# Layer 0's first six steps in orders of their own, bulk loads behind single fetches, and U's and V's split weights first

## The chip, the core and the metric

The kernel runs on one core of one Trainium2 chip. Its time is the device time in microseconds (us) of one execution; the number compared is the median of several runs. One execution was also recorded by the hardware profiler, and every row below is from that one.

## What is computed

The reference takes 32 sequences of 256 token numbers, fetches each token's row of 192 numbers from a table, adds a position row, and runs four layers of a gated recurrence; then one layer of attention with 12 heads and one quantised product. The change touches the fetch and the start of the four layers:

```
x = embedding[tokens] + pos_enc[:S][None]
for l in range(L):                      # L = 4
    h = layernorm(x) * g + b
    uv = h @ Wi.T + bi ; u, v = uv[..., :D], uv[..., D:]        # D = 192
    uc = dwconv_causal(u, cw, cb)                               # 4 taps
    delta = softplus(uc @ wd.T + bd); Bm = uc @ wB.T + bB; Cm = uc @ wC.T + bC
    h_t = h_{t-1} * exp(-delta) + uc * Bm ; y = sum(h_t * Cm)   # over the sequence
    x = x + (y * sigmoid(v)) @ wo.T + bo
```

## The kernel before

The 8192 rows are cut into 16 chunks of two sequences (4 tiles of 128 rows each). Each layer walks over the 16 chunks, and x stays on the chip throughout, so chunk n of layer l+1 needs only chunk n of layer l. The kernel is written with one hand-ordered program for each engine; semaphores tie them together. All of them go through the same sequence of steps (`steps`): in step k of layer 0, `at(j)` is chunk k - j, so one step works on several chunks at different stages. The first six steps and the last few of a layer are written out, those between run in a loop.

The stages of a chunk n, with the engine that does each:

- `index(n)` and `gather(n)`, GpSimd: copies four columns of row numbers and issues four indirect DMAs that fetch the chunk's rows into the buffer `emb`. For the first four chunks (`FIRST`) each has a slot of its own; later chunks reuse slots 0 and 1, and `index(n)` waits until chunk n - 2 was taken out of its slot.
- `place(n)`, VectorE: waits for the fetch, adds the position rows and writes x. `statistics` and `variance` follow.
- `inverse_deviation(n)`, GpSimd: seven small operations that make `rstd`, one of them a power.
- `round_rows(n)`, ScalarE, and `rest_of_rows(n)`, VectorE: the scaled rows `xs`, rounded, and what the rounding left.
- `transposes(n)`, TensorE, and `save_turned(n)`, ScalarE: `xs` turned into `ht`.
- `uv(n)`, TensorE: 15 products with `w_uv` and `w_uv_rest`. `save_u` and `first_tap` on ScalarE and `other_taps` on VectorE make the convolution `uc`; `gates` on ScalarE makes sigmoid(v), `sv_l` and `sv_h`. TensorE's next `uv` waits for the gates of the chunk before, since the banks are the same.
- `round_uc` (ScalarE) and `rest_of_uc` (VectorE), then TensorE's `z_c` and `b_c` with `w_z`, `decay` on ScalarE, `recurrence` on VectorE, `rows` on TensorE, `residual` on VectorE. `bias_rows(n)` on GpSimd adds the output bias to x.

Each layer's weights are prepared one layer ahead: TensorE's `means`, then `centre_weights` (VectorE), `round_weights` (ScalarE) and `split_weights` (VectorE), which computes what rounding left of the weights. For layer 0 this is done ahead of the first step, for layer 1 in steps 2 to 5 of layer 0 (`means(1)` at the end of step 3, once gates(1) is done and layer 1's weights are loaded).

The SyncE program issues the plain loads, in order. After layer 0's weights it waits for the first two fetches, then issues w_o, the four bias rows, all constants of the attention stage and, once `split_weights(0)` is done, layer 1's weights.

## Time and profile before

| | |
|---|---|
| median of 3 runs | 1627.1 us (1626.98 to 1628.12) |
| the profiled execution: its time, its span | 1625.93 us, 1624.1 us |
| TensorE busy | 1522.8 us, 94% of the span |
| VectorE busy | 1345.7 us, 83% |
| ScalarE busy | 1241.7 us, 76% |
| GpSimd busy | 775.8 us, 48% |
| TensorE's mean granted clock | 0.971 of full speed |

The span goes from the first to the last instruction. A row of the waits says who waited for whom, and how long in all. A row of a timeline has the start, the duration, the engine, the line in the kernel, the operation, the tile written and the tile read, how many instructions were merged, and in brackets how long the engine had been idle before it and what ended that. "us to landing" is from a DMA's issue to its completion.

### The profile page before, as it was taken

To read this page: it belongs to the slowest core of one execution; us is meant where nothing else is said; L and a number is where in the kernel's file an instruction comes from. 1 tells how busy PE (TensorE), PEld (TensorE's weight loads), DVE (VectorE), ACT (ScalarE), POOL (GpSimd) and SP (SyncE) were. 2 spreads that over 40 slices of the span, in tenths; PEclk is the share of its full clock that TensorE was granted. 3 is DMA by queue.
4 is the path that set the end of the run, shared out by engine and by line. 5 is a ranking of instruction groups with operands and counts; after the bars stand their busy time and mean duration, and the time that the engine had idled before them with its cause. 6 is when DMAs were issued, how large, how long until landed. Compare 5 with 4: busy or idle time off the path is not lost.

```text
span 1624.1 us, 36462 instructions
## 1 busy us (share of the span) xinstructions
PE 1522.8 (94%) x11337; PEld 1242.0 (76%) x11337; DVE 1345.7 (83%) x3231; ACT 1241.7 (76%) x2686; POOL 775.8 (48%) x1386
## 2 busy tenths in 40 slices
PE   2699999999999999999999998899999999999995
PEld 2478788888888888888788887677777777777763
DVE  4589999889999899999799986678878888788763
ACT  2577878788888788888788884678877878788873
POOL 6655643223333223333233325666666666666542
PEclk9799999999999999999999998899999999999996
DMA  6111110000000000000000000000000000000000
GB/s 156 30 28 22 29 65 1 1 33 0 0 1 1 1 1 0 0 1 1 1 1 0 1 1 1 3 2 17 12 10 10 10 15 11 10 10 10 16 12 25
DMA packets 16572, 22.42 MB, mean 14 GB/s; under 512 B 2912, under 2 KB 13792, under 8 KB 16480
## 3 DMA queue, kind: packets, MB, share of 16 engines
q1 hardware_dynamic: 13408, 14.98, 2.8%
q0 software_dynamic: 3072, 6.30, 2.3%
q8 instruction: 48, 0.79, 0.2%
q14 instruction: 44, 0.36, 0.1%
HBM read 14.58 MB, written 6.29 MB: 13 GB/s over the span
## 4 chain that ended last, share of the span: by engine, by line
PE 41%; ACT 22%; DVE 19%; issue 14%; POOL 2%; DVEq 1%; DMA 1%; ACTq 0%; POOLq 0%
PE banks L861 7%; PE banks L829 6%; PE banks L786 5%; PE banks L813 5%; DVE x L1465 5%; ACT xs L1104 4%; ACT ht L1094 4%; PE banks L800 4%; DVE xs L1376 4%; ACT dc_l L1079 2%; PE banks L637 2%; DVE hs_h L1428 2%; DVE inp_h L1419 2%; PE banks L772 2%; ACT u_h L1050 2%
## 5 line engine op out<-in xcount | busy, mean ns | idle before, releaser
L1521 DVE TENSOR_REDUCE mx<-banks 128x4 f32<-128x1024 f32 x192 | 234.1, 1219 | 44.8 <-PE banks L800 44.2
L1152 ACT ACTIVATE probs<-banks 128x1024 f32<-128x1024 f32 x192 | 195.8, 1020 | 85.3 <-PE banks L813 82.0
L460 POOL TENSOR_TENSOR x<-x,bo_row 128x768 f32<-128x768 f32 (+1 forms) x64 | 118.8, 1856 | 191.6 <-DVE ucr_r L1402 191.6
L637 PE MATMUL banks<-ht,w_uv 128*128 128x512 f32 x576 | 171.8, 408 | 19.5 <-ACT sv_l L1127 13.7
L436 POOL TENSOR_TENSOR lnt<-mv,const 128x4 f32<-128x4 f32 x64 | 20.5, 321 | 315.6 <-DVE mv L1367 315.5
L637 PEld LDWEIGHTS banks<-ht,w_uv 128*128 128x128 f32 x576 | 111.3, 197 | 50.0 <-issue 18.3
L1393 DVE SCALAR_TENSOR_TENSOR uc_h<-u_h,vec,uc_h 128x512 f32<-128x512 f32 x192 | 143.8, 749 | 3.6 <-ACT uc_h L1065 3.6
L1376 DVE SCALAR_TENSOR_TENSOR xs<-x,rstd,xs 128x192 fp32r<-128x192 f32 x256 | 90.0, 413 | 63.8 <-ACT xs L1104 63.8
L1044 ACT ACTIVATE u_l<-banks,vec 64x256 f32<-64x256 f32 x128 | 60.0, 469 | 87.6 <-PE banks L637 86.8
L637 PE MATMUL banks<-ht,w_uv_rest 128*128 128x512 f32 x384 | 122.7, 402 | 0.0
L1061 ACT ACTIVATE uc_l<-banks,vec 64x256 f32<-64x256 f32 x128 | 71.8, 561 | 58.3 <-DVE inp_l L1422 57.2
L813 PE MATMUL banks<-q_t,k_t 64*128 64x256 f32 x768 | 108.9, 333 | 7.0 <-ACT probs L1152 5.1
L646 PE MATMUL banks<-ucr_h,w_z 128*128 128x512 f32 x256 | 107.7, 421 | 6.1 <-ACT ht L1094 5.3
L786 PE MATMUL banks<-identr,parts 128*128 128x128 f32 x768 | 104.3, 260 | 3.9 <-issue 3.0
L1094 ACT ACTIVATE ht<-banks 128x512 fp32r<-128x512 f32 x192 | 100.8, 598 | 4.8 <-PE banks L698 3.3
L698 PEld LDWEIGHTS banks<-identr,xs 128*128 128x128 f32 x768 | 73.8, 142 | 39.7 <-DVE xs L1376 18.1
L1104 ACT ACTIVATE xs<-x,rstd 128x192 fp32r<-128x192 f32 (+1 forms) x256 | 95.6, 444 | 10.8 <-POOL rstd L448 9.2
L829 PE MATMUL banks<-probs,v_aug 128*32 128x256 f32 x1536 | 103.6, 388 | 0.1
L698 PE MATMUL banks<-identr,xs 128*128 128x128 f32 x768 | 76.3, 247 | 29.1 <-DVE xs L1376 18.0
L646 PE MATMUL banks<-ucr_l,w_z 128*128 128x512 f32 x256 | 100.9, 394 | 0.0
L727 PE MATMUL banks<-w_o,sv_h 128*128 128x192 f32 x512 | 100.8, 341 | 0.0
L646 PE MATMUL banks<-ucr_l,w_z_rest 128*128 128x512 f32 x256 | 100.7, 393 | 0.0
(181 smaller groups left out, 4605.2 us busy)
## 6 DMA issues: line engine op xcount, KB each, us to landing
out_dram<-y_out SPq DMA_DIRECT2D x32, 192.0 KB, 2.0
raw_z<-w_z_dram SPq DMA_DIRECT2D x4, 704.0 KB, 6.1
raw_uv<-w_uv_dram SPq DMA_DIRECT2D x4, 576.0 KB, 4.9
emb<-embedding_dram,idx POOLq DMA_INDIRECT x64, 3.6
q_t<-mx_t SPq DMA_DIRECT2D x64, 6.0 KB
emb<-w_qkv_dram SPq DMA_DIRECT2D x1, 864.0 KB, 5.0
w_o<-w_o_dram SPq DMA_DIRECT2D x1, 768.0 KB, 5.5
bo_row<-bout_dram SPq DMA_DIRECT2D x4, 96.0 KB, 7.2
```

What stands on the lines that cost most here:

```text
L637: last = nc.tensor.matmul(out[:], w, r[:], start=(k == 0), stop=(k == len(passes) - 1))
L646: last = nc.tensor.matmul(out[:], w, r[:, b, :], start=(k == 0), stop=(k == len(passes) - 1))
L698: last = nc.tensor.transpose(B_T[g][:, k * P:(k + 1) * P].bitcast(F32R), xs[:, k, g * P:(g + 1) * P], identr[:])
L786: last = nc.tensor.transpose(B_HEADS[g][:, (2 * o + t) * P:(2 * o + t + 1) * P].bitcast(F32R), parts[:, s, t, o, 2 * g:2 * g + 2, :].rearr ...
L813: last = nc.tensor.matmul(B_ST[j][:, t * S:(t + 1) * S], k_t[q, s, g, t * P:(t + 1) * P], q_t[q, s, g, :], start=True, stop=True)
L829: last = nc.tensor.matmul(bank[32 * h:32 * h + 32, c:c + S], v_aug[:, s, t, 4 * p + h, :], probs[:, (s + p) % 2, h // 2, (2 * (h % 2) + t) ...
L1094: last = act.activation(ht[g][:], B_T[g][:], ACT.Identity)
L1104: last = act.activation(xs[:, k, 0:D], x[:, tile_of(c, k)], ACT.Identity, scale=rstd[:, s, k:k + 1])
L1152: act.activation(probs[:, (s + g // 2) % 2, g % 2, :].rearrange("p (j k) -> p j k", j=2), B_SST, ACT.Exp, scale=float(DH) ** -0.5).then_in ...
L1376: last = nc.vector.scalar_tensor_tensor(out=xs[:, k, D:2 * D], in0=x[:, tile_of(c, k)], scalar=rstd[:, s, k:k + 1], in1=xs[:, k, 0:D].bitc ...
L1393: nc.vector.scalar_tensor_tensor(out=uc, in0=uk, scalar=v(l, part, V_W0 + k), in1=uc, op0=ALU.mult, op1=ALU.add).then_inc(taps, 1)
L1521: nc.vector.tensor_reduce(mx[:, s].rearrange("p t (j h) -> p j t h", j=2)[:, :, :, g], B_SS.rearrange("p j (t k) -> p j t k", t=2), AX, AL ...
```

## The change

Four things change, all of them ahead of or within steps 0 to 5 of layer 0; the loops and all later layers keep their order, except that each layer's `split_weights` does U's and V's part first.

1. SyncE: the bias row of layer 0 is loaded behind fetch 1, w_o behind fetch 2, and everything else, layer 1's weights included, behind fetch 3.
2. GpSimd: only fetches 0 to 2 are issued up front, with `inverse_deviation(0)` behind fetch 1 and ahead of fetch 2. In steps 0 to 5 `inverse_deviation(k + 1)` comes ahead of `gather(k + 3)`, and `index(k + 4)` comes last.
3. ScalarE: a first sigmoid on one column stands ahead of everything; layer 0's `w_z` is rounded first, then chunk 0's rows, then `w_uv`; in step 2 gates(0) and round_uc(0) come ahead of round_rows(2).
4. VectorE: steps 0 to 2 have an order of their own (below); in steps 3 to 5 `place(k + 2)` moves from the start of the step to its end. `split_weights` makes `w_uv_rest` first, and TensorE's `uv` waits for these two alone, its `z_c` for all four.

```diff
-            for n in range(2):
-                sp.wait_ge(s_emb[n], 16 * CT)
+            sp.wait_ge(s_emb[1], 16 * CT)
+            sp.dma_start(bo_row[:, 0, :], bout[0:1, :].broadcast_to([P, D])).then_inc(s_bo, 16)
+            sp.wait_ge(s_emb[2], 16 * CT)
             sp.dma_start(w_o[:], w_o_d).then_inc(s_wo, 16)
-            for i in range(L):
+            sp.wait_ge(s_emb[3], 16 * CT)
+            for i in range(1, L):
                 sp.dma_start(bo_row[:, i, :], bout[i:i + 1, :].broadcast_to([P, D])).then_inc(s_wo, 16)
...
-            inverse_deviation(item(0))
+            for n in range(FIRST - 1):
+                wait(pool, s_idx4, n + 1)
+                gather(n, n, n % 2)
+                if n == 1:
+                    pool.wait_ge(s_zero, 3)
+                    inverse_deviation(item(0))
...
+                if l == 0 and k is not None and k < OPENING:
+                    inverse_deviation(at(-1))
+                    if k == 0:
+                        wait(pool, s_idx4, FIRST)
+                    gather(fetched[0], fetched[2], fetched[3])
+                    bias_rows(at(0))
+                    index(indexed[0], indexed[2], indexed[3])
...
                 if first_of_layer(it):
-                    pe.wait_ge(w_split, 4 * (l + 1))
+                    pe.wait_ge(w_split, 4 * l + 2)
...
+            act.activation(table[:], ident[:, 0:1], ACT.Sigmoid)
...
-            round_weights(0)
+            round_z(0)
+            round_rows(item(0))
+            round_uv(0)
...
+                if l == 0 and k == 2:
+                    gates(at(2))
+                    round_uc(at(2))
+                    round_rows(at(0))
...
+            place_and_measure(0)
             centre_weights(0)
+            rest_of_rows(item(0))
+            place_and_measure(1)
             split_weights(0)
...
+                opening = l == 0 and k is not None and k < OPENING
+                if opening and k == 0:
+                    place_and_measure(2)
+                    rest_of_rows(item(1))
+                    return
+                if opening and k == 1:
+                    return
+                if opening and k == 2:
+                    other_taps(at(2), (0, 1, 2))
+                    rest_of_uc(at(2), 1)
+                    rest_of_uc(at(2), 0)
+                    place_and_measure(3)
+                    rest_of_rows(at(0))
+                    place(4, 4, 0)
+                    spread_gain(1)
+                    return
...
                 residual(at(4))
+                if opening:
+                    place(it[0], it[2], it[3])
```

VectorE's program before, from `place(0)` on; `raw_uv` is centring, `w_z_rest` and `w_uv_rest` are the split, `xs` is rest_of_rows(0):

```order
L1332 TENSOR_TENSOR x<-emb,pos 128x768
L1352 BN_STATS stats<-x 128x6 x4
L1367 BN_AGGR mv<-stats 128x2 x4
L1332 TENSOR_TENSOR x<-emb,pos 128x768
L1287 SCALAR_TENSOR_TENSOR raw_uv<-raw_uv,gain,banks 128x384 x3
...
L1307 TENSOR_TENSOR w_z_rest<-raw_z,w_z 128x704 x2
L1310 TENSOR_TENSOR w_uv_rest<-raw_uv,w_uv 128x384 x2
L1332 TENSOR_TENSOR x<-emb,pos 128x768
L1352 BN_STATS stats<-x 128x6 x4
L1367 BN_AGGR mv<-stats 128x2 x4
L1376 SCALAR_TENSOR_TENSOR xs<-x,rstd,xs 128x192 x4
```

The same place in the changed program:

```order
L1368 TENSOR_TENSOR x<-emb,pos 128x768
L1388 BN_STATS stats<-x 128x6 x4
L1403 BN_AGGR mv<-stats 128x2 x4
L1323 SCALAR_TENSOR_TENSOR raw_uv<-raw_uv,gain,banks 128x384 x3
...
L1412 SCALAR_TENSOR_TENSOR xs<-x,rstd,xs 128x192 x4
L1368 TENSOR_TENSOR x<-emb,pos 128x768
L1388 BN_STATS stats<-x 128x6 x4
L1403 BN_AGGR mv<-stats 128x2 x4
L1343 TENSOR_TENSOR w_uv_rest<-raw_uv,w_uv 128x384 x2
L1346 TENSOR_TENSOR w_z_rest<-raw_z,w_z 128x704 x2
L1368 TENSOR_TENSOR x<-emb,pos 128x768
```

Centring no longer stands behind the wait for fetch 1, and rest_of_rows(0) no longer behind the wait for fetch 2.

VectorE's program in step 2 and at the start of step 3, before; the first row is `place(4)`, `uc_l` and `uc_h` are chunk 0's taps, `ucr_l` and `ucr_r` its rest_of_uc, and the last two rows are `place(5)` and chunk 5's statistics:

```order
L1332 TENSOR_TENSOR x<-emb,pos 128x768
L1352 BN_STATS stats<-x 128x6 x4
L1393 SCALAR_TENSOR_TENSOR uc_l<-u_l,vec,uc_l 128x256
...
L1393 SCALAR_TENSOR_TENSOR uc_h<-u_h,vec,uc_h 128x512
L1376 SCALAR_TENSOR_TENSOR xs<-x,rstd,xs 128x192 x4
L1407 TENSOR_TENSOR ucr_l<-uc_l,ucr_l 64x256 x2
L1402 TENSOR_TENSOR ucr_r<-uc_h,ucr_h 128x512
L1279 TENSOR_SCALAR gain_rows<-gain 128x128 x2
L1332 TENSOR_TENSOR x<-emb,pos 128x768
L1352 BN_STATS stats<-x 128x6 x4
```

The same place in the changed program; the two `x` rows are `place(3)` and `place(4)`, and the last row is chunk 4's statistics, the start of step 3:

```order
L1429 SCALAR_TENSOR_TENSOR uc_l<-u_l,vec,uc_l 128x256
L1429 SCALAR_TENSOR_TENSOR uc_h<-u_h,vec,uc_h 128x512
L1443 TENSOR_TENSOR ucr_l<-uc_l,ucr_l 64x256 x2
L1438 TENSOR_TENSOR ucr_r<-uc_h,ucr_h 128x512
L1368 TENSOR_TENSOR x<-emb,pos 128x768
L1388 BN_STATS stats<-x 128x6 x4
L1403 BN_AGGR mv<-stats 128x2 x4
L1412 SCALAR_TENSOR_TENSOR xs<-x,rstd,xs 128x192 x4
L1368 TENSOR_TENSOR x<-emb,pos 128x768
L1315 TENSOR_SCALAR gain_rows<-gain 128x128 x2
L1388 BN_STATS stats<-x 128x6 x4
```

Chunk 0's taps have nothing ahead of them in step 2 now, and the whole of step 3 stands behind `place(4)`. On GpSimd the fetches stood, before, all ahead of the first deviation:

```order
L411 DMA emb<-embedding_dram,idx 128x192 x8
L423 MEMSET const 128x4 x3
L411 DMA emb<-embedding_dram,idx 128x192 x8
L436 TENSOR_TENSOR lnt<-mv,const 128x4
L438 TENSOR_TENSOR lnt<-lnt,const 128x4
```

Now (rows of the deviations between left out; `rstd` is the last operation of each):

```order
L427 MEMSET const 128x4 x3
L419 DMA emb<-embedding_dram,idx 128x192 x8
...
L450 TENSOR_TENSOR rstd<-lnt 128x4
L419 DMA emb<-embedding_dram,idx 128x192 x4
...
L450 TENSOR_TENSOR rstd<-lnt 128x4
L419 DMA emb<-embedding_dram,idx 128x192 x4
L462 TENSOR_TENSOR x<-x,bo_row 128x768
L414 COPY idx<-idx 128x4
```

The deviation of chunk 0 stands behind 8 DMAs where it stood behind 16, and fetches 2 and 3 stand one deviation each later.

## Rows read from the trace of the kernel before

**Rows 1.** Busy time by stretch: start and end us, length, engines, granted clock, DMA share.
```profile
13.20:36.80 23.60, 3.88 (x21) 3.56 (x20) 12.21 (x36) 4.50 (x11) 18.14 (x29) 1.00 0.76 135
...
42.80:55.30 12.50, 0.06 (x1) 0.03 (x1) 9.06 (x24) 7.24 (x15) 10.81 (x16) 0.65 0.21 40
...
158.50:173.70 15.20, 14.28 (x91) 12.18 (x90) 14.38 (x37) 11.80 (x24) 9.12 (x14) 1.00 0.16 26
```

**Rows 2.** Waits from 0 to 76 us: total us, times, longest us.
```profile
DVE x L1332 <- DMA emb<-embedding_dram,idx: 25.8, 6, 8.1
...
PE banks L637 <- ACT sv_l L1127: 12.5, 1, 12.5
```

**Rows 3.** GpSimd's timeline: start us, duration us, line, operation, tile.
```profile
16.25 0.20 POOL L423 MEMSET const<- 128x4 f32 x3
...
20.82 0.95 POOL L411 DMA_INDIRECT emb<-embedding_dram,idx  x1 [0.30 <-issue]
...
25.97 0.95 POOL L411 DMA_INDIRECT emb<-embedding_dram,idx  x1 [0.30 <-issue]
26.94 0.21 POOL L436 TENSOR_TENSOR lnt<-mv,const 128x4 f32<-128x4 f32 x1
...
30.12 0.20 POOL L448 TENSOR_TENSOR rstd<-lnt 128x4 f32<-128x4 f32 x1
...
34.41 1.81 POOL L460 TENSOR_TENSOR x<-x,bo_row 128x768 f32<-128x768 f32 x1
```

**Rows 4.** VectorE's timeline, the same columns.
```profile
13.23 0.96 DVE L1332 TENSOR_TENSOR x<-emb,pos 128x768 f32<-128x768 f32 x1 [8.14 <-DMA emb<-embedding_dram,idx]
...
15.39 0.38 DVE L1367 BATCH_NORM_AGGREGATE mv<-stats 128x2 f32<-128x6 f32 x4
...
24.29 1.02 DVE L1310 TENSOR_TENSOR w_uv_rest<-raw_uv,w_uv 128x384 fp32r<-128x384 f32 x2
29.03 0.96 DVE L1332 TENSOR_TENSOR x<-emb,pos 128x768 f32<-128x768 f32 x1 [3.72 <-DMA emb<-embedding_dram,idx]
...
31.88 1.41 DVE L1376 SCALAR_TENSOR_TENSOR xs<-x,rstd,xs 128x192 fp32r<-128x192 f32 x4 [0.43 <-ACT xs L1104]
37.10 0.96 DVE L1332 TENSOR_TENSOR x<-emb,pos 128x768 f32<-128x768 f32 x1 [3.81 <-DMA emb<-embedding_dram,idx]
...
63.65 0.45 DVE L1393 SCALAR_TENSOR_TENSOR uc_l<-u_l,vec,uc_l 128x256 f32<-128x256 f32 x1
...
65.08 0.75 DVE L1393 SCALAR_TENSOR_TENSOR uc_h<-u_h,vec,uc_h 128x512 f32<-128x512 f32 x1
...
78.24 0.95 DVE L1332 TENSOR_TENSOR x<-emb,pos 128x768 f32<-128x768 f32 x1
```

**Rows 5.** ScalarE's timeline, the same columns.
```profile
30.36 1.49 ACT L1104 ACTIVATE xs<-x,rstd 128x192 fp32r<-128x192 f32 x4 [7.71 <-POOL rstd L448]
...
42.51 0.77 ACT L1065 ACTIVATE uc_h<-banks,vec 128x512 f32<-128x512 f32 x1
...
52.91 1.28 ACT L1127 ACT_TABLE_LOAD   x1
...
69.39 0.63 ACT L1117 ACTIVATE ucr_h<-uc_h 128x512 fp32r<-128x512 f32 x1
...
71.02 0.69 ACT L1130 ACTIVATE sv_h<-banks,vec 128x512 f32<-128x512 f32 x1
```

**Rows 6.** TensorE's timeline, the first product with U's and V's weights.
```profile
36.86 1.62 PE L637 MATMUL banks<-ht,w_uv 128*128 128x512 f32 x3 [1.76 <-ACT ht L1094]
```

**Rows 7.** SyncE's timeline: issues from the loads after w_o to layer 1's.
```profile
19.09 3.05 SPq L357 DMA_DIRECT2D bo_row<-bout_dram  x4
...
31.17 0.79 SPq L349 DMA_DIRECT2D raw_uv<-w_uv_dram  x1
```

**Rows 8.** DMA issues from 0 to 80 us: count, KB each, median us to landing.
```profile
raw_z<-w_z_dram SPq DMA_DIRECT2D x2, 704.0 KB, 7.7
...
emb<-embedding_dram,idx POOLq DMA_INDIRECT x29, 3.6
```

More of the change, by code:

```diff
@@ L89, in build @@
         identr = sb("identr", [P, P], F32R)
+        table = sb("table", [P, 1])
         tok_i = sb("tok_i", [NT, P], I32)
@@ L417, in _ @@
                 index(n, n, n % 2)
-            for n in range(FIRST):
-                wait(pool, s_idx4, n + 1)
-                gather(n, n, n % 2)
-                if n == 1:
-                    for k, value in enumerate((EPS, -0.5, 1.5)):
-                        nc.gpsimd.memset(const[:, k, :], value).then_inc(s_zero, 1)
-                    pool.wait_ge(s_zero, 3)
+            for k, value in enumerate((EPS, -0.5, 1.5)):
+                nc.gpsimd.memset(const[:, k, :], value).then_inc(s_zero, 1)
             LN = 6
@@ L533, in low_parts @@
                 last.then_inc(parts_ready, 1)
-            inverse_deviation(item(0))
-            def step(at, l, k):
-                for lag, stage in ((-4, index), (-3, gather)):
-                    it = at(lag)
-                    if it is not None and it[1] == 0 and (l > 0 or k is None or k - lag >= FIRST):
-                        stage(it[0], it[2], it[3])
-                inverse_deviation(at(-1))
-                bias_rows(at(0))
+            for n in range(FIRST - 1):
[4 more added lines that the diff above has]
+                    inverse_deviation(item(0))
+            def step(at, l, k):
+                indexed, fetched = at(-4), at(-3)
+                if l == 0 and k is not None and k < OPENING:
[5 more added lines that the diff above has]
+                    index(indexed[0], indexed[2], indexed[3])
+                else:
+                    for it, stage in ((indexed, index), (fetched, gather)):
+                        if it is not None and it[1] == 0:
+                            stage(it[0], it[2], it[3])
+                    inverse_deviation(at(-1))
+                    bias_rows(at(0))
                 if l == L and k == 0:
@@ L1199, in step @@
                 save_turned(at(1))
-                round_rows(at(0))
-                round_uc(at(2))
-                gates(at(2))
+                if l == 0 and k == 2:
+                    gates(at(2))
+                    round_uc(at(2))
+                    round_rows(at(0))
+                else:
+                    if not (l == 0 and k == 0):
+                        round_rows(at(0))
+                    round_uc(at(2))
+                    gates(at(2))
                 if (to := prepared(l, k, PREP_ROUND)) is not None:
@@ L1306, in split_weights @@
                 for k in range(2):
-                    nc.vector.tensor_tensor(w_z_rest[:, s, k, :], raw_z[:, k, :], w_z[:, s, k, :].bitcast(F32),
+                    nc.vector.tensor_tensor(w_uv_rest[:, s, k, :], raw_uv[:, k, :], w_uv[:, s, k, :].bitcast(F32),
                                             ALU.subtract).then_inc(w_split, 1)
                 for k in range(2):
-                    nc.vector.tensor_tensor(w_uv_rest[:, s, k, :], raw_uv[:, k, :], w_uv[:, s, k, :].bitcast(F32),
+                    nc.vector.tensor_tensor(w_z_rest[:, s, k, :], raw_z[:, k, :], w_z[:, s, k, :].bitcast(F32),
                                             ALU.subtract).then_inc(w_split, 1)
@@ L1470, in _, with place_and_measure @@
             dve.wait_ge(s_pos, 16)
-            place(0, 0, 0)
-            rows_there(item(0))
-            statistics(item(0))
-            statistics_there(item(0))
-            variance(item(0))
-            place(1, 1, 1)
+            def place_and_measure(n):
+                place(n, n, n % 2)
+                rows_there(item(n))
+                statistics(item(n))
+                statistics_there(item(n))
+                variance(item(n))
+            place_and_measure(0)
             centre_weights(0)
+            rest_of_rows(item(0))
+            place_and_measure(1)
             split_weights(0)
@@ L1606, in step @@
                     centre_qkv(QKV_CENTRE.index(k))
+                opening = l == 0 and k is not None and k < OPENING
[14 more added lines that the diff above has]
+                    return
                 it = at(-2)
-                if it is not None and it[1] == 0:
+                if it is not None and it[1] == 0 and not opening:
                     place(it[0], it[2], it[3])
```

13 lines of the change are left out of this document (11 added, 2 removed).

## Prediction

> **What bounds the kernel now.** I read the busy time by stretch first. In the loop of layer 0 a step takes 15.2 us and VectorE is busy for 14.38 of them, TensorE for 14.28 [rows 1]: both are nearly full, and nothing there is changed. Ahead of it they are not. From 13.2 to 36.8 us TensorE works 3.88 of 23.6 us, and from 42.8 to 55.3 us 0.06 of 12.5, at a granted clock of 0.65 [rows 1]. The opening is a chain of latencies, and a step of the loop can't start before it is through; what the opening gets shorter by, the end should get earlier by, since the engines behind it are full.
>
> The waits say what the chain hangs on. VectorE waits 25.8 us in all for fetched rows, and TensorE once 12.5 us for the gates [rows 2]. The timelines say why. GpSimd issues 16 DMAs in a row, the last at 25.97, and only then (26.94) begins chunk 0's deviation, though its variance is there at 15.39 + 0.38 = 15.77; rstd(0) is ready at 30.32 [rows 3, 4]. So ScalarE's rows of chunk 0 come at 30.36 after 7.7 us of idleness, VectorE's rest of them ends at 33.29, and the first product with U's weights starts at 36.86 [rows 4 to 6]. Fetch 2, last issued at 20.82, is taken at 29.03, and fetch 3, last issued at 25.97, at 37.10, that is 8.2 and 11.1 us, where the median of a fetch is 3.6 [rows 3, 4, 8]. In that time SyncE's bulk loads are in flight: DMA busy 0.76 of the stretch [rows 1, 7].
>
> **The change, step by step.** Durations from the rows: a fetch's four issues 25.97 - 20.82 = 5.15, a deviation 30.32 - 26.94 = 3.4, bias_rows 1.8 and an index copy 0.3 (estimate), place with statistics and variance 15.77 - 13.23 = 2.54, rest_of_rows 1.41, round_rows 1.49 [rows 3 to 5]. From the end of rest_of_rows(0) to the first product 36.86 - 33.29 = 3.57 [rows 4, 6].
>
> *Chunk 0 up to its product.* Fetch 1 was through at 16.25; with the three constants (0.2) now ahead, 16.5. Deviation 0 follows: 19.9. ScalarE has nothing ahead of it: 21.4; VectorE has centred by then (means were done before place(1), and no fetch stands in between now): rest_of_rows(0) 22.9. First product 22.9 + 3.57 = 26.5, against 36.86. `w_uv_rest`: place_and_measure(1) 22.9 to 25.4, then 1.02, 26.4 [rows 4]; just in time, since `uv` waits for these two alone. With the w_z part first it would be 1.7 us later. 10.4 us are won here.
>
> *Chunk 0 up to uc.* GpSimd issues fetch 2 from 19.9 to 25.1, deviation 1 waits for the variance at 25.4 and ends at 28.8, ScalarE's rows 30.3. Chunk 0's last first tap ended 43.28 - 36.86 = 6.4 after its product began [rows 5, 6]; round_rows(1) now stands ahead of save_u(0) until 30.3, which costs some 0.7: 33.6. VectorE meanwhile makes the rest of the weights, place_and_measure(2) and rest_of_rows(1), through at about 32; then nothing stands ahead of the taps: four of them 65.08 + 0.75 - 63.65 = 2.2 and one of 0.7 [rows 4], 36.5. ScalarE turns chunk 1, then gates(0) at once, 33.6 + 1.6 + 1.6 = 36.8, with no table load (1.28 at 52.91 before, [rows 5]), which the one at the start serves; that saving is real at this place and hidden later, so it isn't a term. uc(0) is split at about 39. The 12.5 us of TensorE's idleness shrink to some 3: `uv(1)` needs gates(0) and ht(1), both there by 36.8.
>
> *The price: fetches 3 and 4.* Fetch 3 follows deviation 1: 28.8 to 33.9, last issue 32.9, landed 3.6 later at 36.5; VectorE takes it at 39 with no wait. Then bias_rows(0), index(4), deviation 2: 39.4; fetch 4: 39.4 to 44.5, last issue 43.5. VectorE is done with place_and_measure(3) and rest_of_rows(2) at 43, and stands at place(4), with the whole of step 3 behind it. Fetch 3's landing at 36.5 has just released SyncE's eleven small loads. So what disturbed fetches 2 and 3 before now meets fetch 4. Bounds: undisturbed, 43.5 + 3.6 = 47.1; as late as fetch 3 was, 43.5 + 11.1 = 54.6. Fetch 3 before also stood behind fetch 2, and took 37.10 - 29.03 = 8.1 us for itself under the same load [rows 4]; fetch 4 is alone, so from its first issue 39.4, with some 2 us until data flow (an estimate, between nothing and the 3.6), and 8.1: 49.5. I take 49.5.
>
> *Step 3.* place, statistics and variance 2.54, spread_gain 0.35 (estimate from its small shape), two taps 1.2, four taps 2.2 [rows 4]: 55.8. round_uc's last part 0.63 and the gates 71.71 - 70.02 = 1.7 [rows 5]: 58.1. Before, gates(1) ended at 71.02 + 0.69 = 71.7 and released means(1). TensorE's b_c(0) is through by 54, and layer 1's weights: SyncE took 31.17 - 19.09 = 12.1 us for twelve small issues [rows 7], eleven from 36.5 on make 47.6, the second issue 48.5, landing 7.7 later [rows 8], 56.2, which is 1.9 before they are wanted. So means(1), and with it centring and chunk 0's recurrence, come 71.7 - 58.1 = 13.6 us earlier.
>
> *Steps 4 and 5.* place(6), at 78.24 behind centring [rows 4], stood in a step in which VectorE later waits for ScalarE and TensorE, so it cost nothing; at the end of the step it is exposed, and from place(8) on the count of places is the same as before: 0.95 back. The loop's order is as before. In later layers the two halves of the split only change places, ahead of a step that needs both: nothing.
>
> Sum: 13.6 - 0.95 = 12.7 us off the profiled execution's 1625.93, or 1613.2. The median stands 1.2 above that execution, so 1614.4, rounded 1614.
>
> **A rule against this.** Fetches 2 and 3 before took 8.2 and 11.1 us from last issue against 3.6 [rows 3, 4, 8], so bulk loads hold a fetch up, and here they are only moved onto fetch 4. The Trainium skill, DMA: Bandwidth & Descriptors, section Queues, rings and completion order, says that each DMA engine takes its queues in turn, a packet at a time; by that a fetch beside a full second queue would take twice its time at the most, 7.2 us from last issue, so 50.7 for fetch 4 and 1.2 us more than my sum, 1615.6. The trace only half agrees: 8.2 and 11.1 are more than twice 3.6.
>
> **Rivals.**
> - *Fetch 4 is undisturbed* (47.1). For it: w_o, one large load, has landed by then and only small ones are left. Against it: small ones were in flight too when fetch 3 took 8.1 us [rows 4, 7]. VectorE's chain is 2.4 us shorter, deviation 3 (47 to 50) then nearly bounds: 1612.
> - *The loads strike fully* (54.6), or layer 1's weights come late. The first costs 5.1 us: 1619.5. For the second the margin is 1.9 us; queued behind the small loads and beside fetch 5 they could take 3 to 5 us longer, which costs 1 to 3: 1615 to 1617.
> - *The gain is given back.* Steps 4 and 5 now have each fetch behind a deviation: fetch 8 is issued after deviation 6, which waits for a variance in the middle of step 5, and place(8) opens step 6. From that variance it is 3.4 + 5.15 and 3.6 less the last issue's 1, 11.2 us, until the rows are there, and the rest of a step of 15.2 us and more from its middle, with place(7) and the split of layer 1's weights behind it, is about as long. If every such fetch is 3 us late in steps 3 to 6, four waits make 12 us: 1626, no change.
> - *Slower than before.* One mechanism: place(4) stands in VectorE's program ahead of all of step 3, where before the taps of chunk 1 had a fetch already landed ahead of them. Fetch 4 has to land after 49.5 + 12.7 = 62.2 for a loss, 18.7 us from its last issue; the longest seen is 11.1. At 22 us it would be 1630.
>
> **How the numbers follow.** A measurement of this kernel tells 0.2%, 3.3 us, from no change; faster means below 1623.8. Chances: my forecast, fetch 4 between 48 and 52, 0.45; undisturbed 0.25, which also takes in that TensorE idles less and so runs less at the lower clock (0.65 of full speed in the stretch that shrinks); struck fully or weights late 0.22; given back to within 0.2% 0.05; slower 0.03. The first three are all faster: 0.92. The range reaches from just below the undisturbed case, 1608.5, to just above the struck one, 1620.
>
> **What would show it.** First product with U's weights at about 26.5; rstd(0) at 19.9; chunk 0's uc split at about 39; one table load before the attention stage and none near 37; VectorE waiting at place(4) some 6 us, from 43 to 49.5; means(1) at about 58; the first `inp_h` about 14 us earlier than before and the loop's steps 15.2 us as before. The prediction is wrong if the wait at place(4) is over 12 us, if means(1) waits for raw_z, if place(7) or place(8) wait for fetches, or if the attention stage begins less than 8 or more than 18 us earlier.

## The result and the profile after

Nine runs of the changed kernel have a median of 1625.2 us (1621.56 to 1626.64), nine of the kernel before beside them 1629.25 (1626.98 to 1635.14): a ratio of 0.9971, 95% interval 0.9958 to 0.9984, some 4 to 5 us. The forecast of 1614 and its range from 1608.5 to 1620 are missed. In a later session (12 and 17 runs) the ratio was 0.9988 (0.9972 to 1.0003). By the two sessions the change gains 0.1 to 0.3%, at best a third or so of the 0.8% that was forecast. The profiled execution took 1626.64 us, its span is 1624.8, the longest of its nine.

Busy time by stretch, as in [rows 1]:

```profile
13.20:36.80 23.60, 11.73 (x50) 9.63 (x51) 18.28 (x52) 11.96 (x26) 20.09 (x27) 1.00 0.47 87
42.80:55.30 12.50, 8.40 (x38) 6.76 (x36) 3.67 (x13) 7.87 (x16) 10.33 (x16) 0.73 0.66 171
158.50:173.70 15.20, 14.28 (x90) 12.16 (x90) 14.39 (x36) 11.77 (x25) 9.43 (x14) 1.00 0.15 26
```

The opening is denser (TensorE 11.73 us against 3.88, VectorE 18.28 against 12.21), and the loop's step is what it was. In the second stretch VectorE has fallen from 9.06 to 3.67 us, with a DMA share of 0.66 against 0.21: there it now waits. The waits from 0 to 76 us, as in [rows 2]:

```profile
DVE x L1368 <- DMA emb<-embedding_dram,idx: 16.8, 3, 8.8
...
PE banks L638 <- ACT sv_h L1157: 7.8, 1, 7.8
```

GpSimd's timeline, as in [rows 3] (chunk 0's deviation, fetch 3's last issue, the first bias, fetch 4's last issue, the second bias):

```profile
16.15 0.21 POOL L438 TENSOR_TENSOR lnt<-mv,const 128x4 f32<-128x4 f32 x1
...
18.68 0.20 POOL L450 TENSOR_TENSOR rstd<-lnt 128x4 f32<-128x4 f32 x1
...
33.06 0.95 POOL L419 DMA_INDIRECT emb<-embedding_dram,idx  x1 [0.30 <-issue]
34.04 1.82 POOL L462 TENSOR_TENSOR x<-x,bo_row 128x768 f32<-128x768 f32 x1
...
44.94 0.95 POOL L419 DMA_INDIRECT emb<-embedding_dram,idx  x1 [0.30 <-issue]
...
55.93 1.82 POOL L462 TENSOR_TENSOR x<-x,bo_row 128x768 f32<-128x768 f32 x1
```

VectorE's, as in [rows 4]:

```profile
33.91 2.50 DVE L1429 SCALAR_TENSOR_TENSOR uc_h<-u_h,vec,uc_h 128x512 f32<-128x512 f32 x1 [0.90 <-issue]
...
39.65 0.69 DVE L1438 TENSOR_TENSOR ucr_r<-uc_h,ucr_h 128x512 fp32r<-128x512 f32 x1
40.26 0.95 DVE L1368 TENSOR_TENSOR x<-emb,pos 128x768 f32<-128x768 f32 x1
...
52.89 0.96 DVE L1368 TENSOR_TENSOR x<-emb,pos 128x768 f32<-128x768 f32 x1 [8.80 <-DMA emb<-embedding_dram,idx]
...
55.61 2.70 DVE L1429 SCALAR_TENSOR_TENSOR uc_h<-u_h,vec,uc_h 128x512 f32<-128x512 f32 x1
...
69.63 1.66 DVE L1323 SCALAR_TENSOR_TENSOR raw_uv<-raw_uv,gain,banks 128x384 f32<-128x384 f32 x3 [5.17 <-PE banks L644]
```

TensorE's, as in [rows 6], and where `means(1)` begins:

```profile
25.41 1.62 PE L653 MATMUL banks<-ht,w_uv 128*128 128x512 f32 x3 [1.76 <-ACT ht L1121]
...
63.29 1.65 PE L638 MATMUL banks<-raw_uv,gain_rows 128*128 128x384 f32 x2 [7.80 <-ACT sv_h L1157]
```

SyncE's, as in [rows 7]:

```profile
36.81 1.28 SPq L365 DMA_DIRECT2D bo_row<-bout_dram  x3
...
42.30 0.43 SPq L354 DMA_DIRECT2D raw_uv<-w_uv_dram  x1
42.77 0.43 SPq L355 DMA_DIRECT2D raw_z<-w_z_dram  x1
```

The reader is to see three things. Up to 41 us the milestones come within 1.4 us of the forecast (rstd(0), the first product, uc(0) split). Fetch 4 is taken at 52.9, 8 us after its last issue. And twice `uc_h` takes 2.5 and 2.7 us in place of 0.75, beside a bias addition on GpSimd. And layer 1's weights are issued at 42.3 and 42.8, ahead of fetch 4's last issue, where the forecast had them at 47.6 and 48.5. One place later matters as much, step 5 (VectorE, then GpSimd, then TensorE):

```profile
103.63 0.95 DVE L1368 TENSOR_TENSOR x<-emb,pos 128x768 f32<-128x768 f32 x1
104.49 1.02 DVE L1343 TENSOR_TENSOR w_uv_rest<-raw_uv,w_uv 128x384 fp32r<-128x384 f32 x2
105.43 1.68 DVE L1346 TENSOR_TENSOR w_z_rest<-raw_z,w_z 128x704 fp32r<-128x704 f32 x2
110.48 0.96 DVE L1368 TENSOR_TENSOR x<-emb,pos 128x768 f32 x1 [3.37 <-DMA emb<-embedding_dram,idx]
```
```profile
99.52 0.22 POOL L450 TENSOR_TENSOR rstd<-lnt 128x4 f32<-128x4 f32 x1
...
103.75 4.18 POOL L419 DMA_INDIRECT emb<-embedding_dram,idx  x1 [0.30 <-issue]
```
```profile
112.55 1.21 PE L716 MATMUL banks<-identr,xs 128*128 128x128 f32 x8 [4.93 <-DVE inp_l L1458]
...
115.54 2.89 PE L745 MATMUL banks<-w_o,sv_h 128*128 128x192 f32 x8
```

`place(8)` waits for fetch 8, which stands behind deviation 6 and whose last issue took 4.18 us; TensorE stands idle for 4.93 us, and the eight products of L745 take 2.89 us after that, 1.53 in an undisturbed step.

Where the lead is lost shows best in one milestone, the start of `inp_h` on VectorE, in the recurrence of each of the 64 chunk-and-layer items: 79.1, 114.4, 144.8, 336.8 and 987.5 us for the 1st, 3rd, 5th, 18th and last in the first profile of the kernel before. An item is one chunk in one layer, in the order of the program, so items 1 to 16 are layer 0. The table has each kernel's lead, that is how many us earlier than there its milestone comes (less than nothing: later), for all profiles taken:

| kernel | 1st | 3rd | 5th | 18th | last | median us, and of before beside it | ratio (95%) |
|---|---|---|---|---|---|---|---|
| after | 7.0 | 3.0 | 0.3 | -2.0 | -1.3 | 1625.2, 1629.3 | 0.9971 (0.9958-0.9984) |
| after, 2nd profile | 7.1 | 2.7 | -0.2 | -0.9 | -1.7 | 1626.1, 1626.0 | 0.9988 (0.9972-1.0003) |
| after, 3rd profile | 7.0 | 5.4 | 2.6 | 0.2 | 0.2 | one run, 1624.4 | |
| before, 2nd profile | -1.4 | -0.0 | -3.2 | -4.7 | -5.8 | one run, 1634.1 | |
| e1 loads behind fetch 4 | 14.0 | 11.0 | 10.9 | 9.4 | 3.8 | 1616.5, 1626.5 | 0.9935 (0.9917-0.9953) |
| e2 fetch first | 7.1 | 6.7 | 4.1 | 1.7 | 1.8 | 1619.0, 1626.5 | 0.9947 (0.9926-0.9967) |
| e3 narrow bias | 7.4 | 7.0 | 3.6 | 2.2 | 1.4 | 1624.0, 1627.1 | 0.9975 (0.9960-0.9989) |
| e4 busy TensorE | 9.4 | 8.0 | 5.2 | 2.8 | 2.8 | 1623.1, 1626.5 | 0.9973 (0.9961-0.9986) |
| e5 old steps 3 to 5 | 2.8 | 4.4 | 4.4 | 2.1 | 2.8 | 1622.9, 1626.5 | 0.9983 (0.9969-0.9998) |
| e6 late start | -2.2 | -5.8 | -5.8 | -5.8 | -5.5 | 1637.9, 1627.1 | 1.0061 (1.0039-1.0082) |
| e7 only the loads | -0.9 | -0.5 | -0.6 | -2.3 | -4.0 | 1630.0, 1627.1 | 1.0018 (1.0002-1.0033) |
| e8 e1 and e2 | 13.2 | 11.5 | 8.1 | 6.5 | 5.7 | 1617.5, 1627.1 | 0.9928 (0.9903-0.9953) |
| e9 e8 and busy TensorE | 13.4 | 13.3 | 13.3 | 13.2 | 13.1 | 1615.1, 1626.0 | 0.9927 (0.9906-0.9948) |

From the 5th item to the 16th every kernel keeps its lead within 0.3 us. Up to the 18th item what is lost is lost at four places: fetch 4 and `means(1)`, step 5, the step behind it, and the border to layer 1 (mostly from the 17th to the 18th item). Behind it most keep what they have within some 1 us, but not all: e7 loses 1.7 us more and e1 5.6, of these 3.2 at items 36 and 37 and 1.6 at item 51, among the first items of layers 2 and 3. Its cause is open.

### The profile page after: what moved, and what is told of

It is laid out like the page before. It is cut to its first block, busy times and chain, and to the rows that moved or that the text cites. A ratio compares the mean times of both kernels' runs of the same rounds, so it can differ in the third digit from the quotient of the medians.

```text
span 1624.8 us, 36462 instructions
## 1 busy us (share of the span) xinstructions
PE 1530.0 (94%) x11337; PEld 1247.5 (77%) x11337; DVE 1348.7 (83%) x3231; ACT 1239.3 (76%) x2686; POOL 780.3 (48%) x1386
## 4 chain that ended last, share of the span: by engine, by line
PE 45%; ACT 20%; DVE 18%; issue 13%; POOL 3%; DMA 1%; DVEq 1%; ACTq 0%; POOLq 0%
PE banks L879 7%; PE banks L847 6%; PE banks L804 5%; PE banks L831 5%; DVE x L1501 4%; ACT xs L1131 4%; PE banks L818 4%; ACT ht L1121 4%; DVE xs L1412 3%; PE banks L662 3%; PE banks L653 3%; DVE hs_h L1464 2%; PE banks L790 2%; ACT dc_l L1106 2%; PE banks L903 2%
## 5 line engine op out<-in xcount | busy, mean ns | idle before, releaser
L1429 DVE SCALAR_TENSOR_TENSOR uc_h<-u_h,vec,uc_h 128x512 f32<-128x512 f32 x192 | 147.4, 768 | 3.4 <-ACT uc_h L1092 2.5
L662 PE MATMUL banks<-ucr_h,w_z_rest 128*128 128x512 f32 x256 | 101.0, 394 | 0.0
L745 PE MATMUL banks<-w_o,sv_h 128*128 128x192 f32 x512 | 100.8, 341 | 0.0
L662 PE MATMUL banks<-ucr_r,w_z 128*128 128x512 f32 x256 | 100.7, 393 | 0.0
```

The lines of the kernel that those rows point to most:

```text
L662: last = nc.tensor.matmul(out[:], w, r[:, b, :], start=(k == 0), stop=(k == len(passes) - 1))
L1429: nc.vector.scalar_tensor_tensor(out=uc, in0=uk, scalar=v(l, part, V_W0 + k), in1=uc, op0=ALU.mult, op1=ALU.add).then_inc(taps, 1)
```

## The experiments

**e1, the loads wait for fetch 4.**

```diff
-            sp.wait_ge(s_emb[3], 16 * CT)
+            sp.wait_ge(s_emb[0], 32 * CT)
+            layer_loads(1)
             for i in range(1, L):
...
-                layer_loads(l)
+                if l > 1:
+                    layer_loads(l)
```

> The changed kernel, with everything that SyncE issued behind fetch 3 now behind fetch 4, layer 1's weights first of it. Theory (the bulk loads hold fetch 4 up, 8.0 us from its last issue): place(4) comes at 44.9 + 3.6 = 48.5 instead of 52.9, means(1) at about 59 instead of 63.3 unless layer 1's weights (issued at 48.5, some 7.6 to land, 57) are late, the first inp_h at 68 instead of 72.1; the end 0 to 4 us earlier than the changed kernel's 4 us gain over the kernel before. Rival (fetch 4 is slow for a reason of its own, such as its own issues): place(4) stays near 52.9 and nothing moves. Rival (the opening is absorbed later, whatever it gains): place(4) moves and the time stays at -4 us.

SyncE's first load, and VectorE's places for chunks 4, 5 and 8:

```profile
48.51 0.33 SPq L354 DMA_DIRECT2D raw_uv<-w_uv_dram  x1
```
```profile
48.59 0.96 DVE L1370 TENSOR_TENSOR x<-emb,pos 128x768 f32<-128x768 f32 x1 [4.38 <-DMA emb<-embedding_dram,idx]
...
61.79 0.98 DVE L1370 TENSOR_TENSOR x<-emb,pos 128x768 f32<-128x768 f32 x1 [2.38 <-DMA emb<-embedding_dram,idx]
...
102.50 0.96 DVE L1370 TENSOR_TENSOR x<-emb,pos 128x768 f32 x1 [2.59 <-DMA emb<-embedding_dram,idx]
```

Fetch 4, with its last issue at 45.05, is there 3.5 us later in place of 8.0. The second bias no longer meets `uc_h`; it meets `ucr_l`, which takes 2.92 us in place of 0.86, just ahead of a wait that hides it. TensorE's idle time ahead of `means(1)` falls from 7.8 to 1.1 us, and the first recurrence has a lead of 14.0 us. The price moves on: now fetch 5 is in flight with the loads and `place(5)` waits 2.38. Of the 14, 10.9 are left at the 5th item; `place(8)` waits here too, and TensorE stands idle for 4.1 us, yet nothing is lost in the step behind. So the loads on fetch 4 are the largest single loss at the first recurrence (7 us). The ratio is 0.0036 to 0.0053 below the changed kernel's, 6 to 9 us, more than the 0 to 4 that were expected. The edit does two things, it moves the loads and puts layer 1's weights first among them; the 3.5 us of fetch 4 are the first one's, the share of the second in the rest was not measured alone.

**e2, fetches of steps 3 to 5 ahead of the deviation.**

```diff
+                    if k >= 3:
+                        wait(pool, s_idx4, fetched[0] + 1)
+                        gather(fetched[0], fetched[2], fetched[3])
                     inverse_deviation(at(-1))
...
-                    gather(fetched[0], fetched[2], fetched[3])
+                    if k < 3:
+                        gather(fetched[0], fetched[2], fetched[3])
```

> The changed kernel, with GpSimd's fetch ahead of the deviation again in steps 3 to 5; VectorE's order stays. Theory (fetch 8 is late because it stands behind deviation 6 and its last issue, 4.18 us, behind VectorE's place(7) and split): fetch 8 is issued from about 90, place(8) waits 0 instead of 3.4 us, TensorE does not stand idle for 4.9 us at 107.6 and keeps its clock in steps 6 and 7; chunk 2's inp_h comes about 6.5 us earlier than before instead of 3.0, chunk 4's 6 instead of 0.3, and the end 3 to 6 us earlier than the changed kernel. Rival (the loop takes back any lead): chunk 2 is earlier, chunk 6 is not.

Fetch 8's last issue on GpSimd, and `place(8)`:

```profile
93.73 0.95 POOL L419 DMA_INDIRECT emb<-embedding_dram,idx  x1 [0.30 <-issue]
```
```profile
106.77 0.94 DVE L1372 TENSOR_TENSOR x<-emb,pos 128x768 f32 x1
```

The last issue is 10 us earlier and undisturbed, the wait is gone, and of the loss of 3.7 us in step 5 there are 0.9 left, which is the place that the forecast counted at 0.95. But 2.5 are still lost between the 4th and 5th item (6.6 to 4.1): TensorE stands idle for 2.1 us at the end of step 5 even so, and its granted clock is 0.80 and 0.50 in the two stretches from 104 to 120 us, where it was expected to stay up.

**e3, the bias without its work.** The output bias is added on one column only in the first five chunks of layer 0; the output lacks it there.

```diff
+                if isinstance(n, int) and n < 5:
+                    nc.gpsimd.tensor_tensor(x[:, n * CT * D:n * CT * D + 1], x[:, n * CT * D:n * CT * D + 1],
+                                            bo_row[:, l, 0:1], ALU.add).then_inc(x_biased, 1)
+                    return
```

> The kernel after, with the output bias added on one column only in the first five chunks of layer 0 (the output lacks that bias there), so that GpSimd's 1.8 us additions over 384 columns are gone from the opening. Theory (VectorE's operations with two inputs in SBUF stand still beside GpSimd's bias additions): uc_h of steps 0 and 1 takes 0.74 us in place of 2.50 and 2.70, uc(0) is split at 38.5 us in place of 40.3, place(6) takes 0.95 in place of 2.31; since the means of chunk 1 hang on VectorE's queue behind fetch 4 (still landing at about 52.9), the first recurrence comes 2 to 3.5 us earlier than 72.1, and all of it stands at chunk 8 if the fetches of steps 3 to 5 go out earlier by as much. Time 1622 to 1624 beside the kernel after at 1625. Rival (VectorE waits for fetch 4 whatever it did ahead of it): uc_h is shorter but the first recurrence stays within 0.5 us of 72.1, and the time that of the kernel after within 1 us.

```profile
33.81 0.75 DVE L1433 SCALAR_TENSOR_TENSOR uc_h<-u_h,vec,uc_h 128x512 f32<-128x512 f32 x1 [0.90 <-ACT uc_h L1096]
...
54.50 0.96 DVE L1372 TENSOR_TENSOR x<-emb,pos 128x768 f32<-128x768 f32 x1 [11.51 <-DMA emb<-embedding_dram,idx]
...
57.22 0.74 DVE L1433 SCALAR_TENSOR_TENSOR uc_h<-u_h,vec,uc_h 128x512 f32<-128x512 f32 x1
```

That `uc_h` stretches beside the bias addition is shown: without it both take 0.75. That this moves the first recurrence is not: the rival holds there, 71.7 against 72.1, because fetch 4, issued 1.8 us earlier, landed 1.6 us later (11.4 us from its last issue). SyncE's loads stand in its way wherever VectorE is. The time, 1624.0, doesn't tell the two theories apart. In step 5 `place(8)` doesn't wait here, but the bias addition of chunk 5, which is whole, now meets `w_uv_rest` (3.21 us in place of 1.02), and 2.4 us of the lead go all the same.

**e4, products to keep TensorE's clock.** 34 products of 128x512 into Z's bank, read by nobody, ahead of `means(1)`.

```diff
+                    if l == 0:
+                        wait(pe, decay_ready, 1)
+                        for _ in range(34):
+                            nc.tensor.matmul(B_ZH[:], w_uv[:, 0, 0, 0:HI], ht[0][:], start=True, stop=True)
```

> The changed kernel, with 34 products of 128x512 added on TensorE at the end of step 3, written to a bank that is free and read by nobody, in the 7.8 us in which it waits for gates(1). Theory (the clock falls while TensorE waits, and means(1) and uv(2) then take 6.2 and 4.5 us more than half of it for nothing): the clock stays at 1.0 from 63 to 75, means(1) takes 3.5 us instead of 6.2, chunk 0's inp_h is 2.7 us earlier, and up to that much reaches step 5, where fetch 8 may swallow it. Rival (the clock there doesn't matter): nothing moves.

```profile
63.33 0.91 PE L638 MATMUL banks<-raw_uv,gain_rows 128*128 128x384 f32 x2 [0.95 <-ACT sv_h L1161]
...
66.88 1.65 PE L653 MATMUL banks<-ht,w_uv 128*128 128x512 f32 x3
```

`means(1)` begins at the same time (63.3) and takes 3.5 us in place of 6.2; its first products take 0.91 us against 1.65. Centring starts 2.6 us earlier (67.0 against 69.6) and the first recurrence 2.3, by the clock alone. The products right behind `means(1)` take 1.65 us again: the clock fell there in spite of the added work.

**e5, the old order in steps 3 to 5** (`OPENING = 3`).

```diff
-        OPENING = 6
+        OPENING = 3
```

> The changed kernel, with steps 3 to 5 in the old order on VectorE and GpSimd; steps 0 to 2 keep the new one. Theory: as with the fetch first, and place(5) opens step 3 and place(6) step 4, where it is hidden: place(8) doesn't wait, chunk 2's inp_h 6 to 7 us earlier than before, the end 3 to 6 us earlier than the changed kernel. But place(5) now stands ahead of chunk 1's taps, and its fetch was last issued at 55: it could land at 58 to 59 and cost up to 4 us at the start of step 3. Rival (the loop takes back any lead): the end as the changed kernel's.

```profile
58.49 0.96 DVE L1368 TENSOR_TENSOR x<-emb,pos 128x768 f32<-128x768 f32 x1 [4.47 <-DMA emb<-embedding_dram,idx]
```

`place(5)` stands ahead of the taps again and waits, so the first recurrence leads by 2.8 us only. From there on nothing is lost up to the border: 4.4 at the 3rd item and at the 5th, where the kernel after has 0.3. The order that the change gives to steps 3 to 5 wins about 4 us at their beginning and loses more at their end.

**e6, a late start.** 16 memsets of 128x512 on GpSimd ahead of the first index, each waited for.

> The kernel after, with 16 memsets of 128x512 on GpSimd, each waited for, ahead of the first index: every fetch, and with it the whole opening, starts some 8 to 12 us later (the profile shows how much: D). Theory (the loops pass a shift of the opening on unchanged, and only the named waits of the opening take something back): first recurrence and end both later by D, less what fetch 4 no longer waits for when the loads of layer 0 are done earlier relative to it (none, since the loads of layer 1 still start on fetch 3): time 1625 + D within 2 us. Rival (the rest of the kernel takes shifts up, so an opening is worth less than its size anywhere): the end is later by under half of D, the first recurrence by D.

D is 9.27 us. The first recurrence is 9.2 later than in the kernel after, the third 8.7, the last 4.2, where the kernel after had lost 2.5 and 2.4 on the way that this execution didn't lose. The whole span is 8.0 us longer. The median rose by D or more: the ratios 1.0061 and 0.9971 are 14.6 us apart, those against the second session 11.9, each with an uncertainty of some 4. By the medians and the span a shift of the opening reaches the end, and the rival, that less than half of it does, falls; the last recurrence of this one profile, 4.2 of 9.27, would by itself have spoken for it. Granted clock (last column but two; its two levels are 0.5, that is 1.2 GHz, and 1.00, 2.4 GHz) behind step 5, first in the kernel after, then here, where the same stretch comes some 9 us later:

```profile
112.00:120.00 8.00, 6.21 (x30) 6.01 (x30) 7.84 (x21) 7.34 (x15) 6.23 (x7) 0.54 0.30 51
120.00:128.00 8.00, 8.00 (x38) 7.26 (x39) 7.16 (x17) 3.51 (x8) 3.08 (x8) 0.60 0.00 0
```
```profile
120.00:128.00 8.00, 5.50 (x28) 5.32 (x28) 7.88 (x22) 6.58 (x13) 5.74 (x7) 0.57 0.27 49
128.00:136.00 8.00, 8.00 (x51) 7.00 (x52) 7.20 (x17) 5.22 (x12) 3.60 (x8) 1.00 0.01 3
```

The same work after the same idle time ran at the lower clock through about one stretch in place of two: the 2.5 us behind step 5 are not in the program alone. TensorE's idle time ahead was 4.93 us both times.

**e7, only the loads**, in the kernel before (its SyncE lines of the change, and the two waits for `s_bo` and `s_wo`).

> The kernel before, with the SyncE part of the change alone: first row of the output bias behind fetch 1, W_o behind fetch 2, other rows and the loads of layer 1 behind fetch 3. All five first fetches are out early here and the layer 1 loads come ahead of none of them but the fifth. Theory (the loads cost only where a fetch is issued behind them): no fetch of step 0 is issued later than the loads but that of chunk 5, which is wanted late, so the first recurrence stays within 0.7 us of 79.1 and the time within 2 us of the kernel before. Rival (the early loads held up fetches 0 to 2 in the kernel before): fetch 0 lands over 1 us before 24.3, the first recurrence comes over 1 us earlier, and the time is 1 to 3 us below the kernel before.

```profile
26.65 0.96 DVE L1335 TENSOR_TENSOR x<-emb,pos 128x768 f32<-128x768 f32 x1 [1.40 <-DMA emb<-embedding_dram,idx]
33.06 0.95 DVE L1335 TENSOR_TENSOR x<-emb,pos 128x768 f32<-128x768 f32 x1
48.66 0.96 DVE L1335 TENSOR_TENSOR x<-emb,pos 128x768 f32<-128x768 f32 x1 [9.26 <-DMA emb<-embedding_dram,idx]
```

Fetches 2 and 3 are taken 2.4 and 4.0 us earlier than in [rows 4], fetch 4 8.1 us after its last issue (3.5 in the kernel before) and 2.6 us later than there. I had overlooked that fetch 4 belongs to step 0 here too and runs into the loads. The first recurrence is 0.9 us later (expected: within 0.7), the time 0.18% longer: this part alone gains nothing, it only chooses which fetch pays.

**e8, e1 and e2 together.**

> Both edits together: the loads of layer 1 wait for fetch 4 (its semaphore), and in steps 3 to 5 the fetch goes ahead of the deviation on GpSimd. Theory (losses at named places that add up): lead over the kernel before 14.0 us at the first recurrence as with the first edit alone, and 13.5 to 14.5 still at item 4, where each edit alone leaves 10.9 and 4.1, since chunk 8 is no longer waited for; end of the run 1613 to 1615.5 in place of 1616.5 and 1619.0. Rival (steps 3 to 5 give back 3 us whatever the order, TensorE's lower clock being the cause): lead of about 11 us at item 4 and 1616 to 1617.5.

No wait at `place(8)` (VectorE takes it at 102.04), yet only 8.1 us are left at the 5th item. The expectation of 13.5 and more falls, and it is less than the rival's 11 too. TensorE stands idle for 2.1 and 1.5 us and then has a granted clock of 0.61 and 0.54 in the two stretches from 104 to 120 us:

```profile
104.10 0.88 PE L722 MATMUL banks<-identr,xs 128*128 128x128 f32 x8 [2.09 <-DVE inp_l L1464]
106.50 0.74 PE L722 MATMUL banks<-identr,xs 128*128 128x128 f32 x4 [1.52 <-DVE hc_h L1484]
107.05 2.89 PE L751 MATMUL banks<-w_o,sv_h 128*128 128x192 f32 x8
```

**e9, e8 with a busy TensorE in step 5.**

```diff
+                if l == 0 and k == 5:
+                    wait(pe, sv_ready, at(2)[0] + 1)
+                    for _ in range(9):
+                        nc.tensor.matmul(B_VH[:], w_uv[:, 0, 0, 0:HI], ht[0][:], start=True, stop=True)
```

> The version with both edits (loads of layer 1 behind fetch 4, fetches of steps 3 to 5 ahead of the deviation), and in step 5 nine products of 128x512 into V's bank, which nothing reads, so that TensorE works through its idle time at 101.8 to 104.1 us. Theory (what is left of the loss between the second and the fifth recurrence is TensorE's clock, which fell from 1.00 to 0.61 and 0.54 at 104 to 120 us once TensorE had stood idle): granted clock 0.9 or more at 104 to 120, lead over the kernel before at the fifth recurrence 10.5 to 12 us in place of 8.1, products of L745's kind (step 6) 1.5 us in place of 2.9. Rival (VectorE's two placements and the split of layer 1's weights in a row set the step's length, and the clock only follows): clock high or not, lead at the fifth recurrence 7.5 to 8.6 us. Median time 1614 to 1616 by the first, 1617 to 1618 by the second.

TensorE in step 5 and 6, then the granted clock of 104 to 120 us here:

```profile
94.89 2.32 PE L976 MATMUL banks<-ht,w_uv 128*128 128x512 f32 x9 [0.81 <-ACT sv_h L1167]
...
102.72 0.80 PE L722 MATMUL banks<-identr,xs 128*128 128x128 f32 x8
...
105.02 1.53 PE L751 MATMUL banks<-w_o,sv_h 128*128 128x192 f32 x8
```
```profile
104.00:112.00 8.00, 7.12 (x55) 6.67 (x56) 7.07 (x23) 7.85 (x18) 5.50 (x10) 1.00 0.29 51
112.00:120.00 8.00, 7.18 (x37) 5.57 (x35) 7.97 (x15) 4.68 (x10) 4.36 (x4) 1.00 0.06 12
```

The nine products push the step's own ones back, so that they end when the next are free to start. The clock stays at its upper level, the products of L751 take 1.53 us, and the lead stays at 13.3, and to the end. The lead at the 2nd item was already 14.2 against 12.3 in e8, ahead of the added products, so at most the 3.2 us between the 4th and the 5th item are theirs. The rival (VectorE sets the step, the clock only follows) doesn't fit this profile. But e1 and e6 lose nothing in that step either, without added products, so one profile can't show that the nine products did it. Over all runs e9 (0.9927) is not to be told from e8 (0.9928): whether the profile of e9 is the rule for its program or one execution's luck is open.

**e10, e11 and e12, both kernels profiled again.**

> The kernel after, unchanged, once more with a profile. Theory (what happens up to the sixth chunk is in the program, what TensorE's clock does behind it differs between executions): first recurrence at 72.1, third at 111.4 within 0.3 us again; behind that the losses of 2.5 us between the third and the fifth and of 2.4 us at the border to layer 1 may be there or not. Rival (all of it is in the program): each milestone to the end within 0.5 us of the first profile's. Median time 1622 to 1625.

> The kernel before, unchanged, once more with a profile. Theory (the border to layer 1 is drawn anew in each execution): first recurrence at 79.1 and the item ahead of the border at 322 within 0.3 us again, the next one at 337 or up to 2.5 us later. Rival (the kernel before loses nothing there because of where its steps lie): 336.8 within 0.5 us again.

> The kernel after, unchanged, a third profile. As for the second: the first three recurrences within 0.3 us of 72.1, 90.0 and 111.4; the losses behind them the same each time (all of it in the program) or different (drawn anew).

The kernel after has its first recurrence at 72.1, 72.0 and 72.1 and its wait at `place(8)` of 3.4 us each time. That wait is the same though the third profile reaches step 5 earlier and its last issue takes 3.15 us, not 4.18. VectorE, then GpSimd there:

```profile
103.05 1.68 DVE L1346 TENSOR_TENSOR w_z_rest<-raw_z,w_z 128x704 fp32r<-128x704 f32 x2
```
```profile
102.40 3.15 POOL L419 DMA_INDIRECT emb<-embedding_dram,idx  x1 [0.30 <-issue]
```

The issue ends 0.8 us behind the end of VectorE's `w_z_rest` (105.55 and 104.73), as in the first profile (107.93 and 107.11): it stands until the split is through, however long that is.

 The loss at the border to layer 1 is 2.5, 0.9 and 2.4 us. The third profile leads by 2.4 us more at the 2nd item (9.1 against 6.7): the clock rose earlier (0.95 at 72 to 80 us against 0.80), and `place(6)` took 0.95 us in place of 2.31; so not even the third recurrence (109.0 in place of 111.4) is in the program alone, as I had expected. The kernel before has a second profile 8.2 us longer than the first (span 1632.3): 1.4 us at the first recurrence (made up at the second), 3.0 between the 4th and 5th item, 1.5 at the border and just ahead of it. Its stretch there, where the first profile had a clock of 0.90:

```profile
120.00:128.00 8.00, 8.00 (x37) 7.49 (x36) 7.11 (x22) 6.48 (x14) 4.23 (x9) 0.50 0.15 27
```

So the kernel before can lose 3 us between the 4th and 5th item too, and its first profile, against which the sum was made, is one in which the clock cost little; the first recurrence held less well than expected (80.5).

## Why the prediction was wrong

**What held.** rstd(0) at 18.9 (forecast 19.9), the first product with U's weights at 25.4 (26.5), uc(0) split at 40.3 (39) although `uc_h` took 1.8 us more, since the rest came earlier; one table load, at the start; the loop's step; the loop passes a lead on (e6, and the columns between the 5th and 16th item).

**The sum, term by term.** Forecast was a start of `means(1)` at 58.1, 13.6 us earlier; it began at 63.3 (in the kernel before at 72.3). Fetch 4 came at 52.9 in place of 49.5: 3.4, of these 1.4 by a later last issue (44.9 against 43.5) and 2.0 by a longer flight (8.0 against 6.0). The working took SyncE's pace from the kernel before, 1 us an issue, by which layer 1's weights go out from 47.6 on. At 0.5 us an issue they went out at 42.3 and 42.8, ahead of fetch 4's last issue, so that these two large loads were in flight with it and not only small ones; what they cost apart from the small ones was not measured, since e1 moves all of them. `uc_h` beside the bias: 2.0, a term I didn't have, though both operations and their lengths stand in [rows 3, 4]. Then `means(1)` ran at half the clock: 2.7 us more (e4 gives back 2.6), a term I had only as a chance of gain. The three aren't independent: e1 takes fetch 4's away and with it most of the others, and the first recurrence leads by 14.0. That this is near the forecast's 13.6 is in part luck: `means(1)` begins there at 57.1, a us ahead of the forecast, takes 2.1 us more than in the kernel before, and `place(6)`, 0.9, no longer stands ahead of the first recurrence.

**The steps that failed** are two. *The price: fetches 3 and 4*, with *Step 3* behind it, named the right collision and sized it too low: the first recurrence leads by 7.0 us and not by 13.6, and e1 gives the 7 us back there. *Steps 4 and 5* costed the new order at 0.95 us. That term was right by itself (e2, e8 and e9 lose 0.9 at the 3rd item), but the wait for fetch 8 came on top: the time that the kernel after loses is 3.7 us in step 5 and 2.5 in the step after, in each of its three profiles. The rival of the gain given back described it (fetch 8 behind deviation 6, `place(8)` waiting, with the split of layer 1's weights in between) and got a chance of 0.05 on the ground that the times were about equal. It didn't count that the last issue would stand until VectorE's place and split were through; with the fetch issued earlier, the wait is gone (e2). Nor did it count the lower clock behind TensorE's idle time. That the clock is low where the 2.5 us go is seen in the kernel after, e2, e3, e4 and e8; that a busy TensorE saves them is not shown, since e9 is one profile and e1 and e6 save them without it. One of the prediction's own signs of being wrong came true, `place(8)` waiting for its fetch, and so did another, the attention stage not being 8 us earlier (the last recurrence ahead of it is 1.3 us later); the wait at `place(4)` was 8.8 us, under the 12 it allowed. The premise that the end comes earlier by what the opening gets shorter by holds through the loop of layer 0 (5th to 16th item), and not in every profile across the borders between layers (e1).

**What stays.** At the border to layer 1 the kernel after loses 0.9 to 2.5 us in its three profiles; it lost nothing in e6, in e9 and in the first profile of before. Executions of one program differ by some microseconds there and behind step 5, so the small gains (e3, e4, e5 against after) can't be ranked by their medians. Why e2's median is 4 us below e4's at a like lead is open. That the 4.18 us come from VectorE's three operations is read from rows of three profiles, not from a run without them.

The kernel to keep is e1, e8 or e9, 0.65 to 0.73% below the kernel before, twice and more what the change gave; all have the loads behind fetch 4. Their intervals overlap, so what the fetch ahead of the deviation adds to that is not shown by the times.

## What to carry to other kernels

When an opening is pulled tight, write down for each bulk load which fetch it will now be in flight with: moved off one fetch, it landed here on the next each time (fetch 4 in the changed kernel and in e7, fetch 5 in e1). Look past the part that is reordered, to the step in which the new order meets the old one. A wait that idles TensorE may cost twice, once for itself and once for the lower clock behind it; give the second a range from nothing up to what the same products' durations at either level in rows of the trace make it. And before a loss of 2 or 3 us is laid to the program, profile it more than once.
